# A fused attention and feed-forward kernel: the stacks of the queries issued from two engines and in smaller pieces

## The reference, cut to what matters

```python
x = x + _L0_xattn_ref(_layernorm(x), ctx, mask)        # attention without projections
x = x + _L0_ffn_ref(_layernorm(x), w1, w2, w3)         # ternary weights
x = x + _L1_xattn_ref(_layernorm(x), ctx, mask, Wq, bq, Wk, bk, Wv, bv, Wo, bo, ...)
x = x + _L1_ffn_ref(_layernorm(x), wq_gate, s_gate, wq_up, s_up, wq_down, s_down)

# _L1_xattn_ref, for 8 elements of 112 rows, 375 keys, 16 heads of 32:
q, k, v = proj(hs, Wq, bq), proj(at, Wk, bk), proj(at, Wv, bv)
scores = clip(einsum('bhsd,bhtd->bhst', q, k) / sqrt(32), -50, 50)
probs = softmax(where(attend, scores, -10000))
ctx = einsum('bhst,bhtd->bhsd', probs, v)
```

## Time and profile before

| | us |
|---|---|
| median of 3 runs | 472.57 (471.92 to 473.4) |
| the profiled execution | 470.73 |
| its span | 469.0 |
| PE busy | 443.3 (95%) |
| DVE busy | 316.9 (68%) |
| ACT busy | 245.3 (52%) |
| POOL busy | 109.9 (23%) |
| granted TensorE clock, mean | 0.988 |

### The profile page before, as it was taken

One profiled execution on the slowest core, in us unless ns is written; L12 is line 12 of the kernel. 1 busy time (PEld: TensorE's weight loads), 2 busy tenths in 40 slices (PEclk: granted clock), 3 DMA queues, 4 the chain that ended last, 5 costly groups with the idle time before them and its releaser, 6 DMA issues.

```text
span 469.0 us, 9959 instructions
## 1 busy us (share of the span) xinstructions
PE 443.3 (95%) x3838; PEld 264.2 (56%) x3847; DVE 316.9 (68%) x574; ACT 245.3 (52%) x370; POOL 109.9 (23%) x126
## 2 busy tenths in 40 slices
PE   8989899999899899999998989799999999999997
PEld 6556565655345355554554777577765565555553
DVE  4995596679857887756765467778876976555211
ACT  4755744764566364555754778576745582222000
POOL 2220400025024000000154377543332252000000
PEclk9999999999999899999999999899999999999999
DMA  8999988934695236633489569977342462000111
GB/s 265 326 381 311 367 282 280 323 105 148 211 289 149 60 82 161 187 87 83 71 300 253 184 212 268 280 262 244 115 140 99 123 179 69 0 0 0 41 59 59
DMA packets 59180, 82.73 MB, mean 176 GB/s; under 512 B 20097, under 2 KB 43649, under 8 KB 57985
## 3 DMA queue, kind: packets, MB, share of 16 engines
q1 hardware_dynamic: 59136, 82.14, 56.8%
q10 hardware_dynamic: 2, 0.01, 0.0%
HBM read 58.76 MB, written 14.42 MB: 156 GB/s over the span
## 4 chain that ended last, share of the span: by engine, by line
PE 68%; DVE 14%; SPq 8%; DMA 4%; issue 3%; ACT 1%; POOL 1%; ACTq 0%; DVEq 0%
PE psum L1598 13%; PE psum L208 8%; PE psum L206 8%; PE psum L1648 7%; PE psum L1431 6%; PE psum L1498 4%; PE psum L673 4%; PE psum L1440 3%; PE psum L1545 3%; PE psum L1528 2%; PE psum L1374 2%; SPq L237 2%; DMA w_stage<-in_w 2%; DMA kst<-k_scratch 2%; PE psum L1392 2%
## 5 line engine op out<-in xcount | busy, mean ns | idle before, releaser
L208 PE MATMUL psum<-wv_p,kv_p 128*128 128x512 f16 x288 | 66.1, 379 | 0.5 <-DVE khl L228 0.5
L206 PE MATMUL psum<-kv_p,wk_p 128*128 128x376 f16 x384 | 66.0, 322 | 0.3 <-DVE khl L228 0.3
L1254 ACT ACTIVATE e<-psum,mask_bias 128x448 f32<-128x448 f32 x96 | 53.4, 640 | 14.9 <-PE psum L1528 13.8
L206 PEld LDWEIGHTS psum<-kv_p,wk_p 128*128 128x128 f16 x384 | 37.5, 98 | 24.6 <-issue 0.6
L208 PEld LDWEIGHTS psum<-wv_p,kv_p 128*128 128x128 f16 x288 | 28.0, 98 | 32.9 <-issue 1.2
L1947 DVE TENSOR_SCALAR e<-e 128x1344 f32<-128x1344 f32 x32 | 33.2, 1038 | 9.4 <-ACT e L1254 9.3
L1598 PE MATMUL psum<-xt,wg_b 128*128 128x448 f16 x176 | 36.9, 352 | 0.3 <-issue 0.3
L1545 PE MATMUL psum<-e,vst 128*32 128x112 f32 x768 | 35.2, 267 | 1.9 <-issue 1.1
L1598 PE MATMUL psum<-xt,wu_b 128*128 128x448 f16 x176 | 36.9, 352 | 0.0
L1294 ACT ACTIVATE gated<-psum,gs 128x448 f32<-128x448 f32 x22 | 13.9, 633 | 39.1 <-PE psum L1598 33.5
L355 POOL TENSOR_SCALAR w_stage<-w_stage,w_stat 128x2816 f32<-128x2816 f32 x6 | 17.1, 2850 | 71.8 <-DVE w_stat L350 71.7
(11 more groups left out here) (198 smaller groups left out, 845.5 us busy)
## 6 DMA issues: line engine op xcount, KB each, us to landing
kst<-k_scratch SPq DMA_DIRECT2D x32, 384.0 KB, 5.9
kv_raw<-in_ctx_feat SPq DMA_DIRECT2D x12, 768.0 KB, 6.1
w_stage<-in_w SPq DMA_DIRECT2D x6, 1408.0 KB, 7.9
cn<-in_ctx_tok SPq DMA_DIRECT2D x8, 768.0 KB, 9.4
k_scratch<-khl SPq DMA_DIRECT2D x128, 48.0 KB, 2.4
v_scratch<-vsp SPq DMA_DIRECT2D x24, 256.0 KB, 2.8
vst<-v_scratch SPq DMA_DIRECT2D x8, 768.0 KB, 7.0
qst<-qhl SPq DMA_DIRECT2D x32, 112.0 KB, 5.4
```

What stands on the lines that cost most here:

```text
L206: mm = pe.matmul(psum[:, kv_bank(p), 0:TQ], wk_p[:, u, k, n * P:(n + 1) * P], src[:, v, k, 0:TQ], **ends)
L208: mm = pe.matmul(psum[:, kv_bank(p), :], src[:, u, k, n * P:(n + 1) * P], wv_p[:, v, k, :], **ends)
L1254: act.activation(e[g][:, c, :], psum[:, D_S + (TC * g + c) % 4, 0:4 * S], ACT.Exp, bias=mask_bias[:, b, c:c + 1], scale=1.0 / (WS * QS)).t ...
```

## The change

`queries_stack` gets the engine, the half `u` and the heads as arguments. Half 0: SP issues the four DMAs of u = 0 of each pair, ACT the four of u = 1, for pair 0 right after query_hi(0,2) and for pair 1 right after query_hi(0,3), each behind its own wait for `q_lo`. SP issues the keys of element 1 behind its stacks instead of ahead of them and of the values of element 0. Half 1: its 16 DMAs are spread over the key fetches: two behind each fetch of b = 0 (pair 0), one behind each fetch of b = 1 and b = 2 (pair 1). All of these are issued by SP.

```diff
-        def queries_stack(sp, n, pair):
+        def queries_stack(eng, n, pair, u, heads):
             gs_of = slice(2 * pair, 2 * pair + 2)
-            sp.wait_ge(q_lo, G * n + 2 * pair + 2)
-            for u in range(2):
-                for hh in range(4):
-                    sp.dma_start(qst[n][64 * u:64 * u + 64, hh, gs_of]...,
+            eng.wait_ge(q_lo, G * n + 2 * pair + 2)
+            for hh in heads:
+                eng.dma_start(qst[n][64 * u:64 * u + 64, hh, gs_of]...,
...
+        LATER_STACKS = [(pair, u, hh) for pair in range(2) for u in range(2) for hh in range(4)]
+        STACKS_AT = [LATER_STACKS[2 * i:2 * i + 2] for i in range(G)] + [[s] for s in LATER_STACKS[2 * G:]]
...
             sp.wait_ge(down_sum, TILES)
-            for g in range(G):
-                keys_fetch(sp, 1, g)
             values_fetch(sp, 0, 0)
...
             sp.wait_ge(wq_lo, 1)
-            queries_stack(sp, 0, 0)
-            queries_stack(sp, 0, 1)
+            queries_stack(sp, 0, 0, 0, range(4))
+            queries_stack(sp, 0, 1, 0, range(4))
+            for g in range(G):
+                keys_fetch(sp, 1, g)
             values_fetch(sp, 1, 1)
             for b in range(B):
                 for g in range(G if b + 2 < B else 0):
                     sp.wait_ge(s_sum, TC * (G * b + g + 1))
                     keys_fetch(sp, b + 2, g)
+                    for pair, u, hh in STACKS_AT[G * b + g] if b < 3 else []:
+                        queries_stack(sp, 1, pair, u, (hh,))
                 if b + 2 < B:
                     sp.wait_ge(pv_sum, G * (b + 1))
                     values_fetch(sp, b + 2, b % 2)
-                if b in (1, 2):
-                    queries_stack(sp, 1, b - 1)
...
             query_hi(0, 2)
+            queries_stack(act, 0, 0, 1, range(4))
             turned_hi(6)
             query_hi(0, 3)
...
+            queries_stack(act, 0, 1, 1, range(4))
             query_hi(1, 0)
             query_hi(1, 1)
             exps(0)
```

More of the change, by code:

```diff
@@ L552, in build @@
         ALL_PARTS = parts_until(TILES - 1)
-        def queries_stack(sp, n, pair):
+        def queries_stack(eng, n, pair, u, heads):
             gs_of = slice(2 * pair, 2 * pair + 2)
-            sp.wait_ge(q_lo, G * n + 2 * pair + 2)
-            for u in range(2):
-                for hh in range(4):
-                    sp.dma_start(qst[n][64 * u:64 * u + 64, hh, gs_of].rearrange("p g s -> p (g s)"),
-                                 qhl[n][32 * hh:32 * hh + 32, :, gs_of].rearrange("d v g s -> d v (g s)")).then_inc(q_stacked[n][pair], 16)
+            eng.wait_ge(q_lo, G * n + 2 * pair + 2)
+            for hh in heads:
+                eng.dma_start(qst[n][64 * u:64 * u + 64, hh, gs_of].rearrange("p g s -> p (g s)"),
+                              qhl[n][32 * hh:32 * hh + 32, :, gs_of].rearrange("d v g s -> d v (g s)")).then_inc(q_stacked[n][pair], 16)
+        LATER_STACKS = [(pair, u, hh) for pair in range(2) for u in range(2) for hh in range(4)]
+        STACKS_AT = [LATER_STACKS[2 * i:2 * i + 2] for i in range(G)] + [[s] for s in LATER_STACKS[2 * G:]]
         e = [at(f"e{r}", [P, TC, 4 * S], F32, 56576 + r * 5376) for r in range(4)]
```

## The result

| | before | after |
|---|---|---|
| median of 4 runs | 472.25 us (466.3 to 473.4) | 474.19 us (471.6 to 475.06) |
| ratio, with its 95% interval | | 1.0145 (1.0097 to 1.0193) |
| the profiled execution, its span | 470.73, 469.0 | 471.60, 469.9 |
| PE busy | 443.3 | 442.2 |
| granted TensorE clock, mean | 0.988 | 0.989 |

The ratio leaves disturbed runs out and isn't the quotient of the two medians, which is 1.0041. So it is slower, by 1.1 to 1.5%. The forecast was 0.9% faster, with 0.07 for slower.

The account below looks back on a forecast made before the run. PE was taken as the bound, idling ahead of scores(0) and scores(16). Gains 2.3 + 2.2 = 4.5 us took the profiled 470.73 to 466.2, forecast as 468.1 against the runs' median 472.57; range 465.5 to 471.9.

Parts of the forecast that it names:

- the remaining edits are nearly free: Extra stacks behind key fetches of element 2 take 5.2 us of SP's idle queue; keys still come before they are read.
- ACT stands still during its issues: At pair 0, four ACT issues of 0.64 us delay turned_hi(6) by 2.1 us; PE loses 1.4 us ahead of query(1,0).
- Rival 1: ACT's issues hold up nothing behind them, so query(1,0) isn't delayed; total gain 5.9 us, 466.7 us; chance 0.15.
- Rival 5: With both engines issuing, each issue takes 1.84 us, delaying queries, scores and keys; 6.8 us slower, 479.4 us; chance 0.07.
- Rival 2: Two queues issue at the rate of one, 0.64 us per DMA of either; query(1,0) starts at 251.3; 471.8 us; chance 0.09.
- 2.3 us at the first place: From query(1,0) to scores(2): scores(0) starts 0.80 us earlier, query(1,2) regains 1.49 at full clock; scores(2) moves by 2.29.
- The keys of element 1 are in time: Issued behind the stacks, they land at 260.4 to 262.8 us, scores due at 262.9; cover 2.5 us at the median.
- The wait for the keys of element 4 goes: Ahead of scores(16): keys land at 289.9 to 292.3 us, scores due at 293.70; the 3.04 us wait goes, gain 2.2.
- Rival 4: Interleaved stacks lengthen the landing of element 4's keys beyond 9.7 us of cover; only 2.3 us remain, 470.3; chance 0.10.
- POOL's fold is what is late next: Line 1557 of element 3 waits for the fold of group 1, ending at 299.88 us; gain 2.2 us, not 4.4.
- Rival 6: POOL's fold isn't the next limit, as instructions no longer collide; up to 3.9 us at element 4's keys, 466.4; chance 0.05.
- A gap of 1.8 us is at the edge of free: PE idles about 1.8 us ahead of line 1557; gaps under 1.8 us lose no clock, those over 2.2 do.

Follow-up runs that it names:

- thin stacks: Changed kernel with the half 1 stacks cut from 112 to 2 KB each, every DMA kept; elements 4 to 7 read half 0's stacks; 466.71 us, ratio 0.9989.
- the other execution of before: The kernel before, unchanged, run again for a second trace; median 467.08 us, ratio 0.9996 (0.9956 to 1.0035).
- first place alone: Changed kernel with the half 1 stacks put back behind the values of elements 3 and 4; 468.27 us, ratio 0.9982 (0.9937 to 1.0026).
- order-only run: Also "order alone": kernel before with the keys of element 1 issued behind half 0's stacks, SP issuing all 16; 470.28 us, ratio 1.0037.
- the changed kernel again: The changed kernel, unaltered, measured again beside later experiments; 472.18 us, ratio 1.0108 (1.0054 to 1.0161); its trace is of an execution of 467.53 us.
- second place alone: Kernel before with only the 16 half 1 stacks spread over the key fetches, SP issuing all of half 0; 470.13 us, ratio 1.0072.
- shifted run: Changed kernel with 64 idle matmuls more at its start (128 PE instructions); a single execution of 478.51 us, not compared.
- second place bunched: Kernel before with the half 1 stacks bunched ahead of the value fetches of b = 1 and 2, not behind; 468.84 us, ratio 1.0002.
- stacks ahead of values: Half 1 stacks bunched ahead of value fetches of b = 1 and 2, on the kernel with SP alone issuing half 0's pair 0; 467.33 us, ratio 0.9979.

## Why the prediction was wrong

Two steps failed. The larger is "the remaining edits are nearly free": the eight extra stacks behind the key fetches of element 2 cost 3.8 to 5.3 us between scores(2) and scores(8), by way of PE's own instruction blocks. The other is the sum itself: even without that cost, with thin stacks, the kernel measured 0.9989 (0.9942 to 1.0036) and not 0.991, so the 4.5 us weren't there to be gained. Point by point, in its own order.

**ACT stands still during its issues**: right. I assumed 0.64 us each, and they took 0.71 and, in the second block, 0.80. turned_hi(6) came after 2.25 us of idle time (forecast 2.1), query(1,0) waited 1.64 (forecast 1.4), and no half clock followed. Rivals 1 and 5 fall with the same row. Rival 2 falls too: both engines issued near the rate that SP had alone (medians of 0.61 us on SP and 0.73 on ACT).

**2.3 us at the first place**: the mechanism was right, and the number belonged to one execution. From query(0,0) to scores(2) the profiled execution of before took 24.71 us and the changed kernel 22.57, which is 2.14 less. But the other execution of before took 22.35. It had idled 1.54 us, not 2.22, and paid no half clock. So 1.49 of the 2.3 wasn't there to be gained in it, and the rest was a wait of 1.54 traded for one of 1.64. The step that failed here is the one that took the clock's fall at 256 us for a property of the kernel; of four traces with this first place it came in one. The first place alone measured 0.9982, which agrees with no gain.

**The keys of element 1 are in time**: right for the change; the order-only run shows what ACT's share does for it.

**The wait for the keys of element 4 goes**: right. Rival 4 falls. But the gain was sized by the 3.04 us of one execution, and the other had 1.69. From scores(8) to the last line of element 3 the change gained 1.2 us (28.23 to 27.06) and in the other pair of traces 1.1 (27.40 to 26.32), where I had 2.2.

**POOL's fold is what is late next**: right. PE waited 2.29 us for it. The fold took 3.06 us beside DVE's preparation of Wo, as before. Rival 6 falls. **A gap of 1.8 us is at the edge of free**: a slip. My own numbers give 302.14 - 3.04 - 1.4 = 297.7 for PE's arrival and 299.88 for the fold, so a gap of 2.2 us, which by my own bound has the second cost. The wait was 2.29 us, the clock fell at 302.3 and stayed low for 3.4 us. The first product of `project` took 3.98 us, and its like in before, which ran at the full clock, 2.76. In this execution waiting for POOL thus cost again a part of what the key wait had cost; in the changed kernel again the clock stayed full after 2.30 us, and the same product took 2.76.

**The remaining edits are nearly free**: this is the step that turned the forecast gain into a loss. I priced the stacks behind the key fetches by SP's queue, which had idle time, and asked who reads the keys and when. Both answers hold. What I left out is that the bytes share the DMA engines with PE's own instructions. Eight stacks of 112 KB between the keys and values raised the share of the engines from 0.67 to 1.04 in that stretch, the transfer of the block started 4.4 us after the one before it was entered instead of 1.5, and PE lost 2.97 us in the gap. The section lost 5.3 us in all; the other 2.3 go with the low clock, as the section has no wait for data. That is more than the whole forecast gain. The second place alone turned 2.2 us of forecast gain into a loss of 0.7%.

The sign was there to be read. The timeline of before has two such gaps in the same loop, and I passed over them since they weren't at the places of the change:

```profile
276.89 0.40 PE L1549 MATMUL psum<-e,z_pick_last 128*32 128x112 f32 x8 [1.12 <-issue]
...
288.05 0.29 PE L1545 MATMUL psum<-e,vst 128*32 128x112 f32 x3 [0.78 <-issue]
```

Both are in the middle of the products of one `values(b, g)`, which waits for its exponentials and values only ahead of its first product. I also used the DMA share of 1.09 only to argue that a second queue adds no bandwidth, and didn't ask what else uses those engines.

The Trainium skill (Runtime: NRT & Kernel Launch, Instruction fetch mechanics) says that an engine's instructions come in blocks of 16 KiB, 256 instructions, over a DMA queue, and that the cost of crossing from one to the next is "mostly hidden". The block's size agrees: packets of 16 KB, gaps at multiples of 256. "Mostly hidden" holds in these traces where matmuls are long: outside the loop a single crossing has a gap above 0.2 us, 0.55 in the shifted run. It doesn't hold in the attention loop beside full DMA engines, where between 255 and 305 us about half of the crossings have one, of up to 3.42 us. Had I asked under which load that sentence stops to hold, it would have been the slower rival with the right mechanism.

**The slower rival**: 0.07 for a loss by issue time. The loss came, by another mechanism, and the chance for one that I couldn't name was too low. Nor can 0.3% of the time be told in so few runs: the intervals of the experiments are 0.3 to 0.6% to either side.

**Open.** What exactly holds back the start of a block's transfer when the data queue is full wasn't tried: a place in a queue, or the engines serving the older descriptors first. The 4.7 us behind a single value fetch in before fit the second as well as the first. Nor was it shown how much of the 1% is the gap and how much the low clock behind it; the run with thin stacks removes both at once. That the gap depends on the load is shown by thin stacks against after, and that it belongs to the blocks by the shifted run.

## What to carry to other kernels

Ask of every added or moved transfer not only who reads it and which queue it stands in, but how full the DMA engines are where it lands, because PE's instructions come over them as well; a loop of short matmuls uses up a block of 256 in 4 to 7 us and has little cover. An idle gap without a releaser, where the program has no wait, is the sign: count all of PE's records between such gaps, the sequencer's too, and if the distance is a multiple of 256, look at the instruction queue. And take a second trace before a half clock or a wait of one execution is entered as a gain.

## What the runs showed of the hardware

A block of 256 PE instructions came as one 16 KB transfer of 0.9 to 1.7 us. Between scores(2) and the last line of element 3 it started 0.30 us after the preceding block was entered at the least (order alone, DMA share 0.00), 1.46 in before at a share of 0.79, 0.99 with thin stacks at 1.13, and 3.1 to 5.8 us after it at shares of 1.03 to 1.07 at the four gaps of the changed kernel. In before one transfer started only after 4.74 us at a share of 0.80, with a value fetch issued just ahead. Where PE had been idle at a border, it went on 1.2 to 1.7 us after the transfer's end.

An issue of a 112 KB stack took 0.58 to 0.94 us on ACT (0.71 and 0.80 on average in its two blocks), during which ACT started nothing else, and 0.60 us in the median on SP in before.

The granted clock fell to half, for 3.4 us or twice that, at idle times of PE of 1.69 us (before, another execution), 1.80 and 2.15 (second place alone), 2.22 and 3.04 (before), 2.29 and 2.97 (after). It stayed full after 1.90 (thin stacks), 2.30 (the changed kernel again), 2.36 (second place bunched), 2.54 (stacks ahead of values) and 2.76 (first place alone). So the idle time alone doesn't tell it, and my bound between 1.8 and 2.2 us isn't one.
